# A gated relational graph layer: edge work ahead of the norm, turns of x between segments, gate logits on TensorE

## What is computed

```python
x = (x - mean(x)) / sqrt(var(x) + eps)              # the norm of the rows
w = einsum('rb,bio->rio', att, basis)               # 30 basis matrices of 512x512 into 2 relations
for r in range(2):
    gate = sigmoid(x[src] @ gate_w[r, :, 0])        # the gate logits
    msgs.append(gate[:, None] * x[src] @ w[r])
msg = where(edge_type == 0, msgs[0], msgs[1])
out = segment_sum(msg, dst) + x @ root + bias
```

## Time and profile before

| what | value |
|---|---|
| median of 3 runs | 979.17 us (977.83 to 983.41) |
| the profiled execution, its own time | 982.54 us |
| its span | 980.4 us |
| PE busy | 920.4 us, 94% |
| DVE busy | 621.8 us, 63% |
| ACT busy | 400.0 us, 41% |
| mean granted TensorE clock | 0.982 |
| first segment's first product | 27.52 us |
| first product of `root1`, after the last segment | 162.26 us |

### The profile page before, as it was taken

The page is one execution under the profiler, slowest core; times in us unless marked ns, Lnnn a source line. Parts: engine busy times, 40 slices in busy tenths (PEclk is TensorE's granted clock), DMA queues, the critical chain, the costliest instruction groups (busy, mean ns, idle before and its releaser), DMA issues. The chain is left out here.

```text
span 980.4 us, 12366 instructions
## 1 busy us (share of the span) xinstructions
PE 920.4 (94%) x4576; PEld 609.5 (62%) x4576; DVE 621.8 (63%) x1272; ACT 400.0 (41%) x670; POOL 111.8 (11%) x98
## 2 busy tenths in 40 slices
PE   3889899999999999999998999999999999999997
PEld 1445554674544674488756556989997644545885
DVE  6997988877976842353117652788786524658861
ACT  4877874311113111021113332577875534424540
POOL 0000000000300231100011000253430000023200
PEclk9998999999999999989999999999999999999899
DMA  8979769578712350064976004122004000230001
GB/s 301 337 276 375 262 257 386 205 259 276 240 46 92 133 197 1 0 236 155 320 264 220 3 1 129 49 86 77 11 1 168 5 1 13 80 86 0 1 1 53
DMA packets 63886, 137.31 MB, mean 140 GB/s; under 512 B 6143, under 2 KB 20099, under 8 KB 63810
## 3 DMA queue, kind: packets, MB, share of 16 engines
q1 hardware_dynamic: 62690, 134.95, 39.3%
q0 software_dynamic: 1120, 1.29, 0.5%
HBM read 132.84 MB, written 3.38 MB: 139 GB/s over the span
## 5 line engine op out<-in xcount | busy, mean ns | idle before, releaser
L415 PE MATMUL PS<-AR 128*125 128x512 f32 (+9 forms) x1394 | 394.2, 440 | 9.7 <-DVE AR L1227 1.8
L415 PEld LDWEIGHTS PS<-AR 128*128 128x128 f32 (+3 forms) x1394 | 212.4, 194 | 170.2 <-issue 162.0
L1984 ACT ACTIVATE AR<-PS 128x500 f32<-128x500 f32 (+6 forms) x73 | 41.9, 578 | 153.8 <-PE PS L415 75.6
L1987 ACT ACTIVATE AR<-iota,AR 125x625 f16<-125x625 f16 x119 | 85.9, 812 | 24.6 <-PE PS L502 24.6
L1397 DVE SCALAR_TENSOR_TENSOR AR<-spare,cst,AR 128x512 f32<-128x512 f32 x96 | 69.7, 778 | 13.0 <-DMA spare<-in_rest 12.9
L500 PE MATMUL PS<-AR 125*125 125x512 f16 (+9 forms) x425 | 62.7, 305 | 8.1 <-issue 6.8
L1287 DVE TENSOR_SCALAR AR<-iota,AR 125x625 f16<-125x625 f16 x165 | 60.5, 443 | 12.4 <-PE PS L502 12.3
L500 PEld LDWEIGHTS PS<-AR 125*125 125x125 f16 x425 | 46.7, 143 | 27.7 <-issue 18.8
L2480 POOL TENSOR_TENSOR whl<-AR,whh 128x512 fp32r<-128x512 f32 x32 | 47.7, 1512 | 89.9 <-ACT whh L1984 89.9
L447 PE MATMUL PS<-AR 128*32 128x512 f32 x276 | 41.9, 617 | 16.8 <-DMA AR<-in_basis 15.0
L1832 DVE TENSOR_TENSOR HMl<-AR,HMh 128x626 fp32r<-128x626 f32 x64 | 51.3, 840 | 4.6 <-ACT HMh L1984 4.6
(11 more groups left out here) (325 smaller groups left out, 1507.1 us busy)
## 6 DMA issues: line engine op xcount, KB each, us to landing
AR<-in_basis SPq DMA_DIRECT2D x46, 768.0 KB, 8.8
spare<-in_rest SPq DMA_DIRECT2D x48, 512.0 KB, 4.3
AR<-in_L_ffn_W SPq DMA_DIRECT2D x20, 1024.0 KB, 7.6
spare<-in_basis SPq DMA_DIRECT2D x18, 768.0 KB, 8.5
AR<-in_L_gnn_Wh SPq DMA_DIRECT2D x8, 512.0 KB, 4.1
AR<-in_L_gnn_Wh SPq DMA_DIRECT2D x16, 256.0 KB, 4.8
AR<-in_L_mix_W_qkv SPq DMA_DIRECT2D x4, 768.0 KB, 8.3
AR<-in_L_gnn_root SPq DMA_DIRECT2D x2, 1024.0 KB, 6.5
```

The costliest lines, as they stand in the source:

```text
L415: ins = te.matmul(o, l, r, start=start and i == 0, stop=stop and i == len(pairs) - 1)
L1984: return se.activation(o, i, ACT.Copy, scale=scale)
L1987: return se.activation(o, i, f, bias=bias, scale=scale)
```

## The change

1. On DVE `ends(0)` comes right behind the preparation of the edges, ahead of x; then `imet`, `ends(1)`, and the statistics of the norm. The scaling of x (`ln_scale`, five blocks) comes behind `ends(2)`. On ACT `ends(1)` comes behind `ends(0)`, and the roots behind `ends(2)`.
2. On PE nothing of the norm or the basis is ahead of segment 0. Group 0 of the basis comes after segment 0, and ACT reads it out behind the roots.
3. x is turned block by block after segments 2, 4, 6, 8 and 10 (`TURN`), in the bank `CB`. A turn waits for `w_ready` of all groups before it; the group after it waits until the turn is copied out (blocks 0, 2, 4 by ACT, 1 and 3 by DVE).
4. The gate logits of the first layer are 20 products on PE with 2 columns each, behind segment 12, also in `CB`; ACT makes the sigmoid from there behind `ends(14)`. `gate_rows` goes from DVE's loop, and the load of its weights goes from SP (500 KB written); the weights come as 8 more columns of `cst`. The wait of SP for the logits ahead of the bias loads goes too.

```diff
+AFTER = [0] + [g // 2 + 1 if g % 2 else None for g in range(1, NS - 2)] + [12, 13]
+TURN = {2 + 2 * c: c for c in range(5)}
 FLUSHES = (NS + PER - 1) // PER
...
         halves = [cst[:, 329 + P + h:330 + P + h] for h in range(2)]
...
-        gw = [ar(oB, 2, 512), ar(oB - 374, 2, 512)]
+        gw1 = ar(oB - 374, 2, 512)
...
+        d_x, d_cst, d_iota, d_edge, d_att, d_gw1 = (sem("d_" + n) for n in ("x", "cst", "iota", "edge", "att", "gw1"))
...
                         ins.then_inc(combo_done, 1)
 
             psum.held.add(3)
-            pe.wait_ge(am_ready, 6)
-            combos(0)
-
-
             pe.wait_ge(pool_const, 1)
             pe.wait_ge(flags_ready, 1)
             for i, (b0, b1) in enumerate(((0, 3), (3, 5))):
@@ -463,11 +461,15 @@
                           ind[:, b0:b1, :].rearrange("p b t -> p (b t)"), start=True, stop=True).then_inc(u.sem, 1)
 
 
-            pe.wait_ge(d_cst, 16)
...
+            def turn0(c, groups):
+                pe.wait_ge(d_cst, 16)
                 pe.wait_ge(xn_ready, LN_X + c + 1)
-                turn(("xt", 0, c), c, XN, 4, "dve" if c % 2 else "act")
-
+                pe.wait_ge(w_ready, groups)
+                u = psum.take(("xt", 0, c), "dve" if c % 2 else "act", slot=3)
+                slot(u)
+                for k in range(4):
+                    ins = te.transpose(CB[:, k * P:(k + 1) * P], XN[0:P, c, k * 128:(k + 1) * 128], ident[0:P, 0:P])
...
@@ -503,8 +505,26 @@
                           skip_group_check=True).then_inc(seg_done, 1)
                 if g < NS - 1:
                     te.reg_load(meets[(g + 1) % 2], imet[0:1, g + 1:g + 2])
-                if AFTER[g]:
+                if AFTER[g] is not None:
+                    if g == 0:
+                        pe.wait_ge(am_ready, 6)
+                    if g - 1 in TURN:
+                        read(psum["xt", 0, TURN[g - 1]])
+                    if g == 13:
+                        read(psum["gl"])
                     combos(AFTER[g])
+                if g == 12:
+                    for c in range(NT):
+                        read(psum["xt", 0, c])
+                    pe.wait_ge(w_ready, sum(n is not None for n in AFTER[:g]))
+                    u = psum.take("gl", "act", slot=3)
+                    slot(u)
+                    for c in range(NT):
+                        for k in range(4):
+                            ins = te.matmul(CB[0:P, 2 * c:2 * c + 2], XT[:, k, cols(c)], gwT[:, k, :], start=k == 0, stop=k == 3)
+                    ins.then_inc(u.sem, 1)
+                if g in TURN:
+                    turn0(TURN[g], sum(n is not None for n in AFTER[:g]))
 
...
-            dv.wait_ge(d_x, 16)
-            for c in range(NT):
-                ln_stats(X, 512, c)
-                if c:
-                    ln_scale(X, c - 1, LN_X + c)
-            ln_scale(X, NT - 1, LN_X + NT)
+            def turned0(c):
+                full(("xt", 0, c))
+                ve.tensor_copy(XT[:, :, cols(c)], CB[:, 0:4 * P].rearrange("p (k n) -> p k n", k=4)).then_inc(dve_read, 1)
...
+            dv.wait_ge(d_iota, 16)
+            ends(0)
...
-            for c in (1, 3):
-                turned(("xt", 0, c), c, 4, XT)
-
...
-            dv.wait_ge(d_iota, 16)
-            ends(0)
             ends(1)
+            dv.wait_ge(d_x, 16)
+            for c in range(NT):
+                ln_stats(X, 512, c)
...
-                if g and AFTER[g - 1] and AFTER[g - 1] % 2:
+                if g and AFTER[g - 1] is not None and AFTER[g - 1] % 2:
                     combo_in(AFTER[g - 1])
+                if TURN.get(g - 1, 0) % 2:
+                    turned0(TURN[g - 1])
...
                 if g + 2 < NS:
                     ends(g + 2)
-                if g < NT:
-                    dv.wait_ge(d_gw0, 16)
-                    dv.wait_ge(xn_ready, LN_X + g + 1)
-                    gate_rows(0, g, lambda r: sums[0][:, 0, 1:513])
+                if g == 0:
+                    for c in range(NT):
+                        ln_scale(X, c, LN_X + c + 1)
...
             ends(0)
+            ends(1)
             ac.wait_ge(pool_const, 1)
-            for c in range(NT):
-                ln_root(c, LN_X + c + 1)
-
...
-            combo_out(0)
-            for c in (0, 2, 4):
-                turned(("xt", 0, c), c, 4, XT)
-            ends(1)
             f = 0
...
                 if g + 2 < NS:
                     ends(g + 2)
-                if AFTER[g] and AFTER[g] % 2 == 0:
+                if g == 0:
+                    for c in range(NT):
+                        ln_root(c, LN_X + c + 1)
+                if AFTER[g] is not None and AFTER[g] % 2 == 0:
                     combo_out(AFTER[g])
+                if TURN.get(g, 1) % 2 == 0:
+                    turned0(TURN[g])
+                if g == 12:
+                    full("gl")
+                    act(gate[0:P, :, :], CB[0:P, 0:2 * NT].rearrange("p (c r) -> p c r", r=2), ACT.Sigmoid).then_inc(act_read, 1)
 
 
             def gx_high(lay, r, c):
@@ -2060,9 +2084,7 @@
...
             ac.wait_ge(seg_done, NS)
-            ac.wait_ge(gl_ready, NT)
-            act(gate[0:P, :, :], gl[0:P, :, :], ACT.Sigmoid).then_inc(gate_ready, 1)
-            ac.wait_ge(gate_ready, 1)
+            read(psum["gl"])
 
...
-            def load_gates(lay, d):
-                ye.dma_start(gw[lay][0:P, :, :].rearrange("p r i -> p (r i)"), A["gate_w"][lay:lay + 1, :].to_broadcast([P, 1024])).then_inc(d, 16)
-
...
-                    sp.wait_ge(gl_ready, NT)
...
+        g["L0_gnn_gate_w1"].reshape(2, 4, 128).transpose(2, 1, 0).reshape(128, 8)], axis=1).astype(np.float32)
```

55 lines of the change are left out of this document (28 added, 27 removed).

## The result

| | before | changed |
|---|---|---|
| median of 18 runs, us | 981.33 (977.63 to 991.37) | 987.95 (981.01 to 996.76) |
| ratio, 95% interval | | 1.0062 (1.0042 to 1.0082) |
| span of the profiled execution, us | 980.4 | 988.8 |
| segment 0 / root1 begin at, us | 27.52 / 162.26 | 17.12 / 165.67 |

The changed kernel is slower by 0.6%, some 6 us. The forecast was 978.8, with a range from 972.5 to 985. It stood on a median of three runs, 979.17; over 18 runs the kernel before has 981.33, so 2.2 us of the distance between 978.8 and 987.95 come from that base. The ratios leave out three slow executions (996.76 us here, 990.44 in e10, and 1558.93 in e6 at a mean granted clock of 0.558); medians and ranges hold them.

What follows compares the result with a forecast made beforehand. PE was taken as the bound (94% busy), taking turns with DVE behind 27.5 us. 11.8 - 10.2 - 8.1 + 5.7 = -0.8, plus 1.1, is 0.3 us faster: 979.17 - 0.3 = 978.8 us, range 972.5 to 985.

Steps and rivals of the forecast that it cites:

- That gives segment 0 at 13.0 + 1.1 + 1.6 = 15.7 us: Head: `imet` at 13.0, counts to banks 1.1, start of banks 1.6; segment 0 starts 11.8 us earlier.
- The rival of the clock: Half clock on segment 0 (1.2 us kept) and a stretch as at 90 us (4.5): 984.5 us, slower; chance 0.11.
- I take 4.4: Gate logits on PE in the loop: five blocks cost 4.4 us, between 4.0 and 4.6 by a later stage's rows.
- New waits of PE: Up to segment 13: PE waits newly for ACT, DVE, load 7 and the copies of the turns, together 8.1 us.
- the walk: Up to segments 16 and 17: four engine queues stepped through with row durations, each step at the later of engine and input.
- the walk gives back 1.1 us there: Segments 16 and 17: DVE gets ahead during the gate logits, so 1.1 us of PE's waits vanish; bounds nothing to 4.0.
- 0.3 us faster: Whole kernel: -0.8 us up to segment 13 plus 1.1 behind it, in round numbers nothing.
- From segment 18 on nothing differs: Behind segment 18: flush, `root1` and the loads keep their distances, since each load is released by a group; no change.
- signs of being wrong: Segment 13 before 90 at full clock, `root1` over 5 us off the clock's place, or any step behind 160 us changing length.
- this stretch comes and goes: Profiled execution before: 9 us of half clock behind the second start of the banks, 4.5 lost, taken as not constant.
- A rule weighed: ACT's table changes: 1.3 us each taken; the skill's drain of about 1.38 us per load would give 980.8.

Runs made afterwards that it cites:

- e10: Changed kernel with the 20 narrow gate products in three bursts, behind segments 12, 14 and 16, each copied out by ACT; 978.8 us, ratio 0.9974.
- e6: Changed kernel with gate logits of blocks 0 to 3 as four wide products, block 4 narrow behind segment 14, bias loads later; 984.2 us, ratio 1.0042.
- e1: Changed kernel with 32 products of zeros on PE in the head, 18 ahead of the counts and 14 behind; 986.3 us, ratio 1.0065.
- e15: Kernel of e10 with 32 products of zeros on PE in the head; 982.4 us, ratio 1.0003.
- e8: Changed kernel with 20 products of zeros of 384 columns put between the gate products, four ahead of each block; 988.2 us, ratio 1.0071.
- e3: Kernel before with the gates' part alone: 20 narrow products on PE in one piece, DVE's gate products and their load gone; 988.4 us, ratio 1.0068.
- e4: Changed kernel with ACT's roots and readout of group 0 ahead of its indicators for segment 2; 988.6 us, ratio 1.0072.
- e5: Changed kernel with GpSimd's five additions of bias2 to X moved ahead, to about 211 us; 987.1 us, ratio 1.0039.
- e9: Changed kernel with the broadcast load of 1024 gate weights back ahead of load 5, read by nobody; 989.3 us, ratio 1.0091.
- e16: Changed kernel with all 20 gate products in one piece behind segment 14 instead of segment 12; 989.4 us, ratio 1.0078.
- e14: The kernel of e10 run again, against the kernel before; 979.9 us, ratio 0.9982.
- e11: Kernel of e10 with GpSimd's additions of bias2 moved ahead to 211 us; 978.8 us, ratio 0.9969.

## Why the prediction was wrong

- *"That gives segment 0 at 13.0 + 1.1 + 1.6 = 15.7 us"*: 17.12, and it ended at 21.1 instead of 17.8. The chain to `imet` came as walked (the banks start at 13.97, 14.1 was forecast); the 3.4 us are the pace of the half clock on the banks (3.21 for 1.69) and on segment 0 (3.98 for 2.10). The rival of the clock had segment 0's part alone. e1 and e15 did not win it back in the median.
- *"I take 4.4"*, for the gate logits: at full clock the size was right (4.0 in e8 without the zeros, 4.6 in e10), and the earlier trace rows were the right rows. **The step that failed is this term, because it left the clock out**: eight such rows between wide products are not forty in a row. In one piece they took 5.3 us in the profile, and the granted clock fell inside them for 6.8 us, of which 3.4 are lost; in e3, e4, e5, e9 and e16 a stretch of 10.2 us at the next start of the banks came as well. The forecast asked of the clock only where PE stands still, and here the profile shows PE busy. In three bursts the same products took what the sum said, and the time fell by 8 us.
- *"New waits of PE"*, 8.1 us: up to segment 13 the changed kernel's timeline has 8.9: 1.93, 1.77, 1.84 ahead of groups 1, 2 and 4, 1.46 ahead of group 3, 0.70 at turn 4, and 0.44 and 0.76 at segments 9 and 11. In place and kind nearly as forecast, though the waits behind the first three turns are longer than the walk's 0.7, 1.0 and 1.4; turn 0 and group 6 had none. PE came later to turn 0 than walked: in e10, where it was done with group 0 0.7 us earlier, it waits 1.13 there.
- *"the walk gives back 1.1 us there"*, at segments 16 and 17: the waits of 1.04 and 3.00 became 0.16 and 1.83. They give back 2.05.
- *"0.3 us faster"*, the sum: with the half clock of the gates taken away, e10 and e14 are 2.8 and 1.7 us under the kernel before. That e10 lands on the forecast's own 978.8 is luck: by the table above these two lose 4.1 and 3.4 us less to the half clock than the kernel before, which was not in the sum, and their rest is 2.3 and 2.1 us longer. The sum without the clock was too good by 2 to 3 us.
- *"From segment 18 on nothing differs"*: wrong in the profile, and one of the forecast's own signs of being wrong. PE's wait for a basis load just ahead of root1 is 2.24 us instead of 0.84; and PE waits 3.97 us at 269.8, with 6.8 us of half clock that begin inside this wait. The long wait is DVE's adds beside GpSimd (e5, e11). A sum over the edited stages could not give it; what moving GpSimd's additions won is about 1 us in each pair of medians, less than they can tell.
- *"this stretch comes and goes"*, and the clock's rival at 0.11: the stretches do come and go, but not evenly over the kernels. The kernel before has one of 10.2 us at the start of the banks ahead of segment 12 in its profile; the changed one brings its own at the gates each time. The rival's 984.5 lies 5.3 us above the median that it started from, where 6 were measured: the right direction and nearly the size, but from another stretch than the one at the gates, so this is luck.
- *"A rule weighed"*: the row behind each table load starts within 0.01 us of its end, in the timeline of ACT:

```profile
24.88 1.28 ACT L2005 ACT_TABLE_LOAD   x1
26.17 1.04 ACT L2005 ACTIVATE sd<-mv,eps 125x1 f32<-125x1 f32 x5
27.11 1.24 ACT L2002 ACTIVATE AR<-PS,cst 128x512 f32<-128x512 f32 x2
28.37 1.28 ACT L2005 ACT_TABLE_LOAD   x1
29.66 3.65 ACT L2005 ACTIVATE AR<-iota,AR 125x625 f16<-125x625 f16 x5
```

The drain that the Trainium skill (ScalarE: Activation LUTs, What ACT_TABLE_LOAD costs) adds to each load does not stand behind the load here; the measurement decides for 1.3 us a change.

## What to carry to other kernels

Before small products are moved to TensorE, ask not only how long they take but how long they would run with nothing else among them, and spread them between wide products if the order allows: here that was worth 8 us, while the whole change in its better form is only 2 to 3 us under the kernel before, at the edge of what the runs can tell (0.9974 and 0.9982). When a product's price is taken from rows, ask how many rows one product has: a product of f32 has two. When half clock comes and goes between executions, judge a change by the medians of many runs and by counting the profiles in which a stretch begins at one place, not by one profile. And an engine that gets a new distance to its neighbour can meet GpSimd's work in a stage that was never edited.

## What was new of the hardware

- TensorE's granted clock fell from 2.4 to 1.2 GHz although the profile shows it busy for all of the 3 us ahead (1.00 clock in the window from 94, 0.56 in the one from 97). In those 3 us it did nothing but 128x2 products of f32. In the seven profiles with this piece it stayed down for 3.4 to 6.8 us. The Trainium skill (TensorE: Matmul & The Clock Gate, HAM oscillation — how this bites in real kernels) warns of gaps in which PE stands idle; the fall in the changed kernel has no such gap in front.
- Six DVE additions of 128x512 that read two tensors from SBUF take 4.10 us alone (the kernel before, at 243.77 us) and 7.1 to 9.2 beside GpSimd's additions (7.09 in e14, 9.17 in the changed kernel). The Trainium skill (SBUF — State Buffer, SBUF: two separate sides) says that such an instruction and one of GpSimd that reads SBUF exclude each other at a shared port pair for their whole length. The trace agrees: one add takes up to 1.82 us beside GpSimd in the changed kernel and 0.75 alone.
- Products of zeros that bring PE up ahead of a stage moved the half clock on by some microseconds and did not shorten the median (e1, e15).
